# Two alternating places in PSUM for the groups of a graph layer's aggregation, with its one-hot matrices copied in and its gathers written out

## What is computed

```python
h = (x @ W1).reshape(n, 8, 96)
ex = exp(leaky_relu(al_s[src] + al_d[dst]) - m[dst])   # one weight per edge and head
z = segment_sum(ex, dst)
out = segment_sum(h[src] * (ex / z[dst])[:, :, None], dst) + bias
```

## Time and profile before

| what | us |
|---|---|
| median of 3 runs | 2793.61 |
| lowest and highest run | 2791.96 to 2797.63 |
| the profiled execution | 2813.5 |
| its span, first to last instruction | 2811.7 |
| TensorE (PE) busy | 1794.2 (64%) |
| GpSimd (POOL) busy | 1264.5 (45%) |
| VectorE (DVE) busy | 1248.1 (44%) |
| ScalarE (ACT) busy | 806.2 (29%) |
| granted TensorE clock, mean | 0.773 |

### The profile page before, as it was taken

How to read it: one execution, slowest core, us unless ns; L and a number is a source line. 1 busy time by engine, 2 the same in 40 slices (tenths; PEclk the granted TensorE clock), 3 DMA queues, 4 the chain that set the end, 5 groups by cost and what they waited for, 6 DMA issues and landing times. The chain is left out here.

```text
span 2811.7 us, 45815 instructions
## 1 busy us (share of the span) xinstructions
PE 1794.2 (64%) x14517; PEld 1177.2 (42%) x14518; DVE 1248.1 (44%) x2621; ACT 806.2 (29%) x2172; POOL 1264.5 (45%) x1248
## 2 busy tenths in 40 slices
PE   2747668755555556555678935555555568899970
PEld 1324445433333333333344513333333356677750
DVE  7625658465656556566475051111111126221216
ACT  2400001323333333343122413333333332233320
POOL 4065561076767667710411256666666600112116
PEclk9968889956667566778899966676666777899995
DMA  5313221287877778851797988989898972445549
GB/s 184 97 41 74 68 48 35 95 256 248 253 247 250 254 250 254 261 190 45 189 251 195 259 251 303 316 308 309 306 314 312 315 259 103 129 163 163 165 175 403
DMA packets 185256, 586.03 MB, mean 208 GB/s; under 512 B 40189, under 2 KB 56572, under 8 KB 184930
## 3 DMA queue, kind: packets, MB, share of 16 engines
q0 software_dynamic: 87216, 374.99, 43.4%
q1 hardware_dynamic: 72626, 140.92, 14.9%
q10 hardware_dynamic: 25344, 69.32, 6.4%
HBM read 482.25 MB, written 96.45 MB: 206 GB/s over the span
## 5 line engine op out<-in xcount | busy, mean ns | idle before, releaser
L1437 PE MATMUL acc<-ring,work 128*32 128x192 f32 x1952 | 183.6, 489 | 149.1 <-ACT work L1495 73.3
L1373 POOL DMA_INDIRECT ring<-feat_tab,islot x196 | 231.7, 1182 | 95.7 <-issue 45.7
L1631 PE MATMUL acc<-ring,work 128*32 128x192 f32 (+1 forms) x1952 | 172.7, 494 | 124.6 <-issue 90.7
L862 PE MATMUL acc<-wg,work 128*128 128x384 f32 x600 | 232.1, 532 | 24.2 <-issue 17.4
L1553 POOL DMA_INDIRECT ring<-feat_tab,src_t x196 | 195.3, 996 | 111.9 <-issue 51.8
L1179 PE MATMUL acc<-wg,work 128*128 128x384 f32 x600 | 215.6, 509 | 24.0 <-ACT work L1236 21.5
L812 POOL DMA_INDIRECT edges<-score_tab,src_p x168 | 165.0, 982 | 127.7 <-PE tps L850 56.2
L1410 DVE TENSOR_TENSOR ring<-ring,edges 128x768 f32<-128x768 f32 x196 | 183.0, 956 | 81.7 <-DMA ring<-feat_tab,islot 72.5
L1441 PEld LDWEIGHTS acc<-edges,work 128*32 128x32 f32 x982 | 151.2, 155 | 110.8 <-issue 11.8
L1631 PEld LDWEIGHTS acc<-ring,work 128*32 128x32 f32 x1952 | 90.9, 148 | 184.6 <-issue 168.5
L1631 PE MATMUL acc<-work 128*32 128x192 f32 x1104 | 98.4, 470 | 98.1 <-issue 68.9
(11 more groups left out here) (378 smaller groups left out, 3743.5 us busy)
## 6 DMA issues: line engine op xcount, KB each, us to landing
slot_out<-ring SPq DMA_DIRECT2D x57, 384.0 KB
feat_tab<-work ACTq DMA_DIRECT2D x50, 384.0 KB
ring<-lo_rows SPq DMA_DIRECT2D x49, 256.0 KB
edges<-in_w_slow SPq DMA_DIRECT2D x28, 384.0 KB, 9.9
edges<-in_w_hebb POOLq DMA_DIRECT2D x28, 384.0 KB, 7.7
edges<-in_w_fast POOLq DMA_DIRECT2D x28, 384.0 KB, 9.4
unit_sum<-edges SPq DMA_DIRECT2D x28, 384.0 KB, 6.7
agg_raw<-work ACTq DMA_DIRECT2D x25, 388.0 KB
```

The costliest lines, as they stand in the source:

```text
L862: m = nc.tensor.matmul(acc[:, sl * 2 + c, 0:C // 2], xT[sl][:, k, :], wg[:, k, c * (C // 2):(c + 1) * (C // 2)], start=(k == 0), stop=(k = ...
L1373: pool.indirect_dma_start(rows[k][:, 0:C], None, feat_tab[l], bass.IndirectOffsetOnAxis(ap=islot[:, h * UN + k:h * UN + k + 1], axis=0)).t ...
L1437: m = nc.tensor.matmul(sums_ps[c * WIN:(c + 1) * WIN, 0:CHUNK], hot, row[:, c * CHUNK:(c + 1) * CHUNK], start=start, stop=True, skip_group ...
L1631: m = nc.tensor.matmul(sums_ps[c * WIN:(c + 1) * WIN, 0:n], hot, row[:, c * CHUNK:c * CHUNK + n], start=start, stop=True, skip_group_check ...
```

## The change

- *Two places.* The groups alternate between bank 0 and bank 1 of `acc`. TensorE keeps the bank of the open group in a register (`bank_reg`, the group's number mod 2); since the addresses are constants, the matmuls of a tile are there twice, and a branch on the register picks one (`added`, `opened`). An opening waits until the group before the last has been copied (`flushed` begins at 1). ScalarE copies out of PSUM straight into `raw`, with no staging tile; the tile `stage[0]` serves as the second place for a group's one-hot, so `next_hot` runs two groups ahead. Its stream is written out.
- *One-hots.* VectorE makes them for a whole turn (14 tiles) at once into `big` (`made`), one turn ahead of the rows, and SyncE copies each half turn into the small tile when TensorE is past it.
- *Gathers.* GpSimd's 392 are written out, with indices straight from `src_t`; `islot` and its counts go.

```diff
-            sums_ps = acc[:, 0, 0:CHUNK + ZC]
+            next_x = [onehot_x, stage[0][:, 0:WIN]]
             hot_x = hot_open.rearrange("p (b n) -> p b n", b=NW)
+            hots = big[:, 0:NT * WIN].rearrange("p (t n) -> p t n", t=NT)
...
-                    with pool.Fori(0, TURNS // 2 - 1) as i:
-                        for h in range(2):
-                            pool.wait_ge(idx_ready, i * 2 + (h + 2))
-                            for k in range(UN):
-                                pool.wait_ge(tile_mm, i * (2 * UN) + (h * UN + k + 2))
-                                pool.sem_inc(tick_p, 1)
-                                gather(k, 1 - h)
...
+                    for t in range(NT):
+                        k = t % UN
+                        if t >= UN:
+                            pool.wait_ge(tile_mm, t - UN + 2)
+                        pool.indirect_dma_start(rows[k][:, 0:C], None, feat_tab[0],
+                                                bass.IndirectOffsetOnAxis(ap=src_t[:, t:t + 1], axis=0)).then_inc(row_in[k], 16)
+
+                @block.sync
+                def _(sp):
+                    sp.wait_ge(hot_made, 1)
+                    for j in range(2):
+                        sp.dma_start(onehot[:, j * BATCH:(j + 1) * BATCH, :], hots[:, j * BATCH:(j + 1) * BATCH, :]
+                                     ).then_inc(hot_in[j], 16)
+                    for i in range(1, TURNS):
+                        sp.wait_ge(hot_made, i + 1)
+                        for j in range(2):
+                            first = i * UN + j * BATCH
+                            sp.wait_ge(batch_mm, i * 2 + j)
+                            sp.dma_start(onehot[:, j * BATCH:(j + 1) * BATCH, :], hots[:, first:first + BATCH, :]
+                                         ).then_inc(hot_in[j], 16)
...
+                    def made(i):
+                        V.tensor_tensor(hots[:, i * UN:(i + 1) * UN, :], near.to_broadcast([P, UN, WIN]),
+                                        dst_rel[:, i * UN:(i + 1) * UN].unsqueeze(2).to_broadcast([P, UN, WIN]),
+                                        ALU.is_equal).then_inc(hot_made, 1)
...
+                    made(1)
+                    for i in range(TURNS):
+                        if 0 < i < TURNS - 1:
+                            made(i + 1)
+                        messages(i)
...
-                            m = nc.tensor.matmul(sums_ps[c * WIN:(c + 1) * WIN, 0:CHUNK], hot, row[:, c * CHUNK:(c + 1) * CHUNK],
+                            m = nc.tensor.matmul(acc[c * WIN:(c + 1) * WIN, bank, 0:CHUNK], hot, row[:, c * CHUNK:(c + 1) * CHUNK],
                                                  start=start, stop=True, skip_group_check=True)
...
+                    def added(i, k, t, bank):
+                        if k % BATCH == 0:
+                            pe.wait_ge(hot_in[k // BATCH], i * 16 + 16)
+                        pe.wait_ge(msg_ready, t + 1)
+                        sums(onehot[:, k, :], k, t, bank, False).then_inc(tile_mm, 1)
+
+                    def opened(b, k, t, bank):
+                        pe.wait_ge(open_ready, b)
+                        pe.wait_ge(flushed, b)
+                        sums(next_x[bank], k, t, bank, True).then_inc(open_mm, 1)
...
                         for k in range(UN):
                             t = i * UN + k
-                            if k % BATCH == 0:
-                                pe.wait_ge(hot_ready, i * 2 + (k // BATCH + 1))
-                            pe.wait_ge(msg_ready, t + 1)
-                            sums(onehot[:, k, :], k, t, False).then_inc(tile_mm, 1)
+                            bank = pe.snap(bank_reg, min_val=0, max_val=1)
+                            with pe.If(bank > 0):
+                                added(i, k, t, 1)
+                            with pe.Else():
+                                added(i, k, t, 0)
                             with pe.If((bits & (1 << k)) > 0):
                                 close()
                                 pe.load(regs, bend[0:1, ds(t, 2)])
                                 b0, b1 = [pe.snap(r, min_val=j, max_val=NW - 2 + j) for j, r in enumerate(regs)]
                                 with pe.Fori(b0 + 1, b1 + 1) as b:
-                                    pe.wait_ge(open_ready, b)
-                                    pe.wait_ge(flushed, b)
-                                    sums(onehot_x, k, t, True).then_inc(open_mm, 1)
+                                    pe.reg_mov(bank_reg, b & 1)
+                                    bank = pe.snap(bank_reg, min_val=0, max_val=1)
+                                    with pe.If(bank > 0):
+                                        opened(b, k, t, 1)
+                                    with pe.Else():
+                                        opened(b, k, t, 0)
...
+                    def next_hot(q):
+                        if q < NW:
+                            if q >= 3:
+                                act.wait_ge(open_mm, q - 1)
+                            nc.scalar.activation(next_x[q % 2], hot_open[:, q * WIN:(q + 1) * WIN], ACT.Copy).then_inc(open_ready, 1)
+                    act.sem_inc(flushed, 1)
...
                             act.wait_ge(closed, q + 1)
-                            nc.scalar.activation(stage[w % 2], sums_ps, ACT.Copy).then_inc(flushed, 1)
-                            next_hot(q + 2)
-                            act.wait_ge(flushed, q + 1)
                             for c in range(4):
-                                nc.scalar.activation(raw[sl][w * WIN:(w + 1) * WIN, c * CHUNK:(c + 1) * CHUNK],
-                                                     stage[w % 2][c * WIN:(c + 1) * WIN, 0:CHUNK], ACT.Copy)
...
+                                nc.scalar.activation(raw[b % 2][w * WIN:(w + 1) * WIN, c * CHUNK:(c + 1) * CHUNK],
+                                                     acc[c * WIN:(c + 1) * WIN, q % 2, 0:CHUNK], ACT.Copy)
+                            nc.scalar.activation(raw[b % 2][w * WIN:(w + 1) * WIN, C:ROW], acc[0:WIN, q % 2, CHUNK:CHUNK + ZC],
+                                                 ACT.Copy).then_inc(flushed, 1)
+                            next_hot(q + 3)
```

More of the change, by code:

```diff
@@ L1352, in aggregate @@
         def aggregate():
-            H, l = HEADS[0], 0
+            H = HEADS[0]
             L = "_a0"
             row_in = [sem(f"row_in{k}" + L) for k in range(RING)]
[L1356 to L1359, removed]
+            hot_in = [sem(f"hot_in{j}" + L) for j in range(2)]
+            msg_ready, hot_made, open_ready, tile_mm, open_mm, table_ready = (
+                sem(n + L) for n in ("msg", "hot_made", "open_hot", "tile_mm", "open_mm", "open_table"))
+            closed, flushed, zero_set, batch_mm = (sem(n + L) for n in ("closed", "flushed", "zero_set", "batch_mm"))
             st_out = [sem(f"st_out{j}" + L) for j in range(2)]
@@ L1396, in _ @@
+                    made(0)
                     V.tensor_tensor(hot_x, near.to_broadcast([P, NW, WIN]),
                                     dst_open[:, :].unsqueeze(2).to_broadcast([P, NW, WIN]), ALU.is_equal).then_inc(table_ready, 1)
-                    def hots(i, j):
-                        V.tensor_tensor(onehot[:, j * BATCH:(j + 1) * BATCH, :], near.to_broadcast([P, BATCH, WIN]),
-                                        dst_rel[:, ds(i * UN + j * BATCH, BATCH)].unsqueeze(2).to_broadcast([P, BATCH, WIN]),
-                                        ALU.is_equal).then_inc(hot_ready, 1)
@@ L1405, in messages @@
-                    def messages(i, j):
-                        for k in range(j * BATCH, (j + 1) * BATCH):
-                            dve.wait_ge(row_in[k], i * 16 + 16)
-                            r3 = rows[k][:, 0:C].rearrange("p (h c) -> p h c", h=H)
-                            V.tensor_tensor(r3, r3, ex[:, ds(i * UN + k, 1), :].rearrange("p a h -> p h a").to_broadcast([P, H, C // H]),
-                                            ALU.mult).then_inc(msg_ready, 1)
-                    def indices(i, h):
-                        V.tensor_copy(islot[:, h * UN:(h + 1) * UN], src_t[:, ds(i * UN, UN)]).then_inc(idx_ready, 1)
@@ L1417, in turn @@
-                    def turn(i, h, first=False, last=False):
-                        for j in range(2):
-                            if not first:
-                                dve.wait_ge(batch_mm, i * 2 + j)
-                            hots(i, j)
-                            if j == 1 and not last:
-                                indices(i + 1, 1 - h)
-                            messages(i, j)
-                    turn(0, 0, first=True)
-                    with dve.Fori(0, TURNS // 2 - 1) as i:
-                        turn(i * 2 + 1, 1)
-                        turn(i * 2 + 2, 0)
@@ L1478, in _ @@
                 def _(act):
[L1479 to L1491 removed]
+                    def next_hot(q):
[4 more added lines that the diff above has]
```

(7 more changed lines are left out.)

53 lines of the change are left out of this document (16 added, 37 removed).

## The result

The changed kernel takes 2816.07 us (median of 4 runs, 2813.95 to 2818.39), before beside it on the same chip 2795.62 (4 runs, 2791.96 to 2801.34): ratio 1.0066, 95% interval 1.0049 to 1.0084, so slower by 0.7%, some 20 us. The profiled execution took 2815.87 us, span 2814.1.

A forecast was written before the change was run, and what follows sets the result against it. It took layer 0's chain of close, copy, open on TensorE (658 us) as the bound. Sequencer 424 + 161 + 72 = 657 and 15 left over made 672: some +13 on the 2793.6 median, 2806 us, range 2735 to 2848.

The forecast's parts named there:

- The new sum: Layer 0 stage after the change: TensorE's sequencer 424 + 161 + 72 = 657 us, new chain 672 against 658.
- what was left over: Layer 0 time beyond the sequencer's 657 us: 10 us for late counts and 5 for missing rows at the start.
- The price of the If: TensorE's sequencer, each of 392 tiles: register copy 0.10, branch 0.21, half a jump 0.10; 0.41 us, 161 in all.
- The jump without a compare: TensorE's jump over the If's other half: taken as 0.20 us between 0.05 and 0.27, so 0.10 a tile.
- The first rival: TensorE's If bookkeeping is cheap, register copy folded or jump 0.05 us: kernel 2757 or 2769, 2720 with both; chance 0.26.
- Openings: TensorE, layer 0: old turns 27, a wait 3, 99 openings 147 us; the change adds 0.73 an opening, 72 us.
- Late counts: Counts over 4.4 us late still stop TensorE's openings; ten could cost 1 to 2 each: 10 us, between 0 and 20.
- GpSimd's waits: In layer 0 after the change, GpSimd would wait about 80 us for tiles, its gathers needing 584 us.
- The clock: TensorE's array wants 0.74 us a tile at 1.2 GHz, the sequencer 1.04, so the lower clock's 33 us go.
- the account of before: Old layer 0 stage as a TensorE chain of 658 us: sequencer 424, lower clock 33, VectorE 13, late copies 188.
- the 188 us for late copies: Missing part of the old layer 0 chain, put down to ScalarE's late copies; nearly all would go with two places.
- gathers become the bound: If TensorE's sequencer asks for less, GpSimd's 584 us of gathers set layer 0: 604 for 670, kernel 2728; chance 0.10.

The follow-up runs named there:

- weights-in-the-row kernel: The changed kernel with a tile's 8 weights copied behind its row by VectorE and the fifth matmul removed; 2548.96 and 2551.72 us, ratios 1.0087 and 1.0080 to before.
- one place: The kernel before with one-hots made ahead and gathers written out, but no second place and no If; 2533.52 us, ratio 1.0013 to before.
- late copies: The kernel before with three unread ScalarE copies ahead of the real copy in every second group; 2532.68 us, ratio 1.0019 to before.

## Why the prediction was right, and where it wasn't

The forecast, 2806 us and slower by some 13, was 10 under the result. **The new sum** held, on the first chip and on the prompt one: it had 657 for the sequencer and 672 with what was left over; first load to the end of the last copy is 563.8 to 1231.9, 668 us. (Its terms for an opening add up to 1.50 us, not 1.48, and 2793.6 with 13.7 more is 2807; neither matters.)

- *The price of the If.* 0.41 a tile was right: the tiles show 0.37 and 0.46 over 0.63, 0.41 on the mean, and the steps, start to start, 0.09 + (0.26 + 0.12 + 0.23)/2 = 0.39. The jump without a compare, put at 0.20 between 0.05 and 0.27, is 0.23 start to start. The first rival (bookkeeping cheap) needed under 0.375: the register's copy stands alone in 364 tiles, and the jump costs nearly as much as a compare that jumps. The two figures of the Trainium skill (Advanced Engine Details and Errata, section Control Flow Timing), 51 ns for a jump always taken and 108 ns for compare and branch, are not borne out: the rows have 0.17 us for the first, and for the second 0.20 to 0.21 where it jumps and 0.07 where it falls through.
- *Openings.* What is left of the stage, 665.9 less 392 x 1.045 (196 tiles on either side), is 256 us for 99 openings and 28 turns. The prediction had 177 + 72 = 249.
- *Late counts.* 10 us left over, between 0 and 20. TensorE waits 1.6 us for ScalarE in one place, and the stage differs by 2 us between the chips: near 0. As predicted, a copy has a group to arrive. For rows the prediction had 5 us; 31 are put down to them, 7.3 of these at the start.
- *GpSimd's waits* for tiles are 110.3 us where 80 were forecast, and VectorE never waits for TensorE, as forecast.
- *The clock.* Predicted was that the sequencer's 1.04 us a tile covers the array's 0.74 at the lower clock, and so it does, though all of the stage runs at 0.50 and not a mix.

**The step that failed is the account of before.** The prediction called its stage a chain on TensorE, 424 + 33 + 13 + 188, in which the 188 us for late copies lie on the path and would go. On a prompt chip these 188 are gone without the change, and the stage is not 470 but 583.6. Between the sequencer's chain and the 657 stood the gathers, with 584 us by the prediction's own sum, given to a rival with 0.10 as the bound of the kernel after, and never set against the kernel before. What could be had by curing the late copies was at most 74 us, not 188, and the If put the sequencer's chain some 82 us over the gathers' line (664 to 666 against 582 to 584): 0.7% slower on a chip that has the lateness, 3.6% on one without. The total came out right since the new sum stands by itself, and the difference was taken against before's measured time, not against the account of it. That the difference, +13 forecast and +20 measured, came out as well was luck: it needed a before of 2796 us again, and in all the experiments before takes 2528 to 2533, where the same change costs 90. A sum that is made to agree by a remainder (188 was what was missing) proves nothing about what the remainder is. The check at hand was to set the remainder against each other engine's own sum: the gathers alone need 584 us of the 658, so no cure of a wait on TensorE could give more than 74.

The rival *gathers become the bound* comes near only in the weights-in-the-row kernel: a stage of 590 to 592 us where its price was 604.

Open stays why TensorE's counts come late on the first chip and not on the prompt one, how stops of 7 us rather than 3 get through to GpSimd, and whether the changed kernel saw fewer late closes there (0.42 us on the mean against 1.70) for its second place or for its slower dispatch. On the first chip both kernels also lose 80 us ahead of the stage, so what slows them isn't the stage's own. No run tried the other way to a second place, one matmul whose address in PSUM comes from a register.

## What to carry to other kernels

Before removing a wait, add up each engine that would take its turn next, and set it against the stage as it is, not only as it will be: here a gather engine at 584 of 658 us left 74 us to win, and the If that freed the wait cost more. A place chosen at run time by an If in every tile costs about 0.4 us of TensorE's sequencer a tile (register copy, branch, half a jump), some 1.6 us a group here, far more than the copy of 0.34 us per group that it hides. Where the old kernel's time moves by 10% from chip to chip, a change has no single ratio: the changed stage was the same to 2 us, and the old one moved by 74. And before giving the price of a tile, look at both sides of a branch: three tiles in a row showed only the cheaper one.

## What the hardware showed that I had not expected

- A count alone on TensorE's queue (51 ns in its row) costs 0.15 us of the time to the next step: three of them make 176 us in 392 tiles.
- The side of an If that is fallen into is the dearer one: its compare takes 0.12 us instead of 0.26, start to start, but the jump over the other half takes 0.23, so a tile takes 1.09 us instead of 1.00.
- One small matmul with an address step costs the sequencer 0.17 us in a tile (1.00 and 1.09 us with them, 0.83 and 0.92 without).
- The clock granted to TensorE is 0.50 all through the stage in every kernel here whose tiles come evenly 1.0 us or more apart, but 0.59 to 0.71 on the mean where they come quickly (0.63) with stops between them. Before, one place and late copies, each over its stage or most of it:

```profile
480.00:1070.00 590.00, 398.77 (x5110) 257.34 (x5110) 391.76 (x474) 218.43 (x698) 456.78 (x390) 0.59 0.85 278
```

```profile
490.00:1060.00 570.00, 383.31 (x5040) 248.83 (x5035) 380.42 (x413) 211.85 (x678) 449.41 (x386) 0.60 0.89 295
```

```profile
486.00:1070.00 584.00, 348.54 (x5110) 232.28 (x5110) 390.52 (x474) 341.64 (x845) 449.95 (x389) 0.71 0.85 279
```

  and the changed kernel on a prompt chip:

```profile
480.00:1150.00 670.00, 455.11 (x5110) 288.75 (x5110) 389.15 (x419) 166.74 (x594) 450.39 (x392) 0.50 0.80 254
```

- One kernel, 2796 us in one place and 2532 in another, with the same gathers (1.18 us on the mean in both) and the same copies (0.34 us): what differs in the stage is when one engine's work follows another's, 1.70 us from close to copy against 0.07.
